# The last five steps of an image, issued in another order on every engine, in a fused attention-and-convolution kernel

## What is computed

```
xn = group_norm(x)                       # one group a channel
q, k, v = conv3(xn_windows, qw|kw|vw)    # 3x3, in windows of 16x16, then folded to 64 tokens of 128 features
q, k, v = layer_norm(q|k|v)
att = softmax(q k' + bias_table)         # 8 heads, 64 tokens
xr  = xn + unfold((att v) @ proj_w.T + proj_b)
y   = xr + conv3(gelu(conv3(xr, c1w, c1b)), c2w, c2b)      # 3x3 over the whole image
out = x + y
```

## Time and profile before

| | |
|---|---|
| time, median of 3 runs (lowest, highest) | 811.29 us (810.05, 811.31) |
| the profiled execution's own time | 810.2 us |
| its span in the trace | 808.4 us |
| mean granted TensorE clock | 0.993 |
| PE busy | 744.3 us, 92% |
| DVE busy | 657.2 us, 81% |
| ACT busy | 569.1 us, 70% |
| POOL busy | 491.9 us, 61% |

### The profile page before, as it was taken

One profiled execution on the slowest core, in us unless ns is written; L12 is line 12 of the kernel. 1 busy time (PEld: TensorE's weight loads), 2 busy tenths in 40 slices (PEclk: granted clock), 3 DMA queues, 4 the chain that ended last, 5 costly groups with the idle time before them and its releaser, 6 DMA issues.

```text
span 808.4 us, 18167 instructions
## 1 busy us (share of the span) xinstructions
PE 744.3 (92%) x5898; PEld 549.4 (68%) x5898; DVE 657.2 (81%) x2150; ACT 569.1 (70%) x1191; POOL 491.9 (61%) x1041
## 2 busy tenths in 40 slices
PE   0469999999899999999899999999999999999988
PEld 0247877777556778877555778777655688787753
DVE  6549889897859899897967989899775989887675
ACT  1399888767367988876547978876737788878630
POOL 6368778741457788763346777874244778886210
PEclk9999999999999999999999999999999999999999
DMA  7112331000013161000101332100101314000002
GB/s 266 59 30 60 96 144 60 2 1 23 38 65 97 33 239 44 18 1 1 59 33 54 110 125 116 60 1 2 56 5 66 98 32 135 2 2 2 2 1 104
DMA packets 17662, 47.32 MB, mean 59 GB/s; under 512 B 2080, under 2 KB 2720, under 8 KB 17568
## 3 DMA queue, kind: packets, MB, share of 16 engines
q1 hardware_dynamic: 17568, 46.15, 16.7%
HBM read 37.76 MB, written 8.39 MB: 57 GB/s over the span
## 4 chain that ended last, share of the span: by engine, by line
PE 67%; DVE 12%; ACT 9%; issue 5%; POOL 5%; DMA 0%; SPq 0%; POOLq 0%; ACTq 0%; DVEq 0%
PE y_ps L1015 18%; PE o_bank L1081 9%; PE s_ps L1056 8%; PE pt_ps L1069 7%; PE y_ps L982 4%; PE s_ps L1097 3%; PE t_ps L1040 3%; PE ox_ps L1138 3%; PE o_bank L1138 3%; PE pt_ps L1138 3%; PE s_ps L1138 3%; PE y_ps L1010 2%; DVE h_lo L505 2%; DVE h_hi L502 2%; ACT qk_n L855 1%
## 5 line engine op out<-in xcount | busy, mean ns | idle before, releaser
L743 POOL TENSOR_TENSOR sc<-sc,mx 128x512 f32<-128x512 f32 x128 | 133.7, 1044 | 59.9 <-DVE mx L568 59.9
L855 ACT ACTIVATE qk_n<-y_ps,ln_nr,ln_rs 128x128 f32<-128x128 f32 x256 | 104.4, 464 | 88.4 <-POOL ln_nr L733 88.2
L1015 PE MATMUL y_ps<-w_hi,x_hi 128*128 128x192 f16 (+1 forms) x512 | 147.2, 287 | 0.0
L1015 PE MATMUL y_ps<-w_hi,x_lo 128*128 128x192 f16 (+1 forms) x512 | 146.9, 287 | 0.0
L1015 PE MATMUL y_ps<-w_lo,x_hi 128*128 128x192 f16 (+1 forms) x512 | 146.7, 287 | 0.0
L541 DVE BATCH_NORM_STATS2 ln_st<-y_ps 128x6 f32<-128x128 f32 x384 | 88.8, 287 | 60.1 <-PE y_ps L1015 58.9
L1081 PE MATMUL o_bank<-v_bd,pt 128*128 128x66 f32 x1024 | 129.1, 269 | 3.9 <-DVE on L589 3.8
L1081 PEld LDWEIGHTS o_bank<-v_bd,pt 128*128 128x128 f32 x1024 | 124.4, 192 | 5.5 <-DVE pt L575 4.7
L730 POOL TENSOR_TENSOR ln_rs<-ln_ve,neg_half 128x3 f32<-128x3 f32 x128 | 113.4, 886 | 10.7
L870 ACT ACTIVATE sc<-sc 128x512 f32<-128x512 f32 x128 | 82.8, 647 | 39.3 <-POOL sc L743 39.3
L863 ACT ACTIVATE v_bd<-y_ps,ln_vs 128x128 f32<-128x128 f32 x256 | 105.2, 475 | 0.0
(11 more groups left out here) (190 smaller groups left out, 1607.7 us busy)
## 6 DMA issues: line engine op xcount, KB each, us to landing
xs<-in_x_sh_dram SPq DMA_DIRECT2D x32, 576.0 KB, 4.4
xst<-in_x_al_dram SPq DMA_DIRECT2D x16, 512.0 KB, 8.2
xf<-in_x_al_dram SPq DMA_DIRECT2D x32, 256.0 KB, 5.2
out_dram<-xf SPq DMA_DIRECT2D x32, 256.0 KB, 2.0
wst<-in_wqkv_dram SPq DMA_DIRECT2D x1, 768.0 KB, 4.2
w1s<-in_w_dram SPq DMA_DIRECT2D x1, 256.0 KB, 8.7
w2s<-in_w_dram SPq DMA_DIRECT2D x1, 256.0 KB, 8.7
biasS<-in_bias_t_dram SPq DMA_DIRECT2D x1, 256.0 KB, 9.6
```

The source lines that it names most:

```text
L743: pool.tensor_tensor(sc[i % 4][:, :, :, :], sc[i % 4][:, :, :, :], mx[i % 2][:, :, :].unsqueeze(2).to_broadcast([P, HP, TOK, 2]), ALU.subt ...
L855: ins = act.activation(qk_n[j][:, t, :].rearrange("p (h y x) -> p h y x", h=HEADS, y=2), by_head(y_ps[j][:, E * t:E * (t + 1)]), ACT.Identity,
L1015: ins = pe.matmul(y.rearrange("p (t e) -> p t e", t=3)[:, :, cols], xx[r % 2][:, s, a % 2, 2 * TS * (a // 2):2 * TS * (a // 2 + TS)], ww[: ...
```

## The change

Steps 32 to 36 are taken out of `steps` (which now ends at step 31), and each engine gets a function `tail` with the same work in another order. The bodies of the single jobs move into functions of their own and are otherwise as they were.

- PE: the transposes by key and outputs of the last pairs stand ahead of the tiles of the first convolution. Before, the order was c1(4), c1(5), by_key(30), outputs(29), project(6), c1(6), c1(7), by_key(31), outputs(30), by_feature(28), (29), c1(8), outputs(31), by_feature(30), c1(9), by_feature(31), project(7), c1(10), convolution of the next image's pair 0, c1(11), c1(12).
- The convolution of the next image's pair 0 stands ahead of c1(10) (`head` no longer issues it).
- The banks are dealt out anew: tiles 4 to 12 take `t_ps`, y0, y1, s0, s1, `t_ps`, s0, s1, `pt_ps`; project(6) takes the halves of `s_ps` like the projections before it, project(7) `ox_ps` and `o_bank`; c2(0) and c2(1) take s0 and s1. The waits follow.
- DVE: the copy, division and additions of the last pairs are spread between the `low` of the tiles: two `low` ahead of the last division, four between the next image's `row` and the last addition, four after it, then the border.
- ACT: the next image's `high` and the last `copy_ot` are interleaved with the read-outs of the tiles; `split(7)` stands ahead of the read-out of tile 9.
- POOL: `inverse` stands ahead of `split(5)`; the next image's four `low` stand between `split(6)` and `split(7)`, as before.

```diff
-            for i in range(HEAD.stop, PAIRS + 5):
+            for i in range(HEAD.stop, PAIRS):
...
-        c1_in = {28: (0,), 29: (1,), 30: (2,), 31: (3,), 32: (4, 5), 33: (6, 7), 34: (8,), 35: (9,), 36: (10,)}
+        c1_in = {28: (0,), 29: (1,), 30: (2,), 31: (3,)}
-        c1_bank = [t_bank if t == 10 else c_ps[t % 2 if t < 4 else (t + 2) % 4] for t in range(T1N)]
-        c2_bank = [c_ps[3], c_ps[2], pt_bank, o_bank[:, :], ox_ps[:, :], pt_bank, o_bank[:, :], ox_ps[:, :]]
-        proj_bank = [[s_ps[:, w, 256:512] for w in range(2)] for r in range(6)]
-        proj_bank += [[ox_ps[:, 0:256], t_bank[:, 0:256]], [ox_ps[:, 0:256], pt_bank[:, 0:256]]]
+        y0, y1, s0, s1 = c_ps
+        c1_bank = [y0, y1, y0, y1, t_bank, y0, y1, s0, s1, t_bank, s0, s1, pt_bank]
+        c2_bank = [s0, s1, pt_bank, o_bank[:, :], ox_ps[:, :], pt_bank, o_bank[:, :], ox_ps[:, :]]
+        proj_bank = [[s_ps[:, w, 256:512] for w in range(2)] for r in range(NROW - 1)]
+        proj_bank += [[ox_ps[:, 0:256], o_bank[:, 0:256]]]
...
-        low_in = {32: (0, 1, 2, 3), 33: (4, 5), 35: (6, 7, 8)}
...
+            def tail(b, p0, r0, followed):
+                copy_pt(30, p0)
+                normalise(29, p0)
+                if followed:
+                    row_scales(b + 1)
+                    start_scales(b + 1)
+                copy_pt(31, p0)
+                normalise(30, p0)
+                add_rows(6, b, r0)
+                low(b, 0)
+                low(b, 1)
+                normalise(31, p0)
+                if followed:
+                    for r in range(2):
+                        row(r, r0 + NROW)
+                for t in range(2, 6):
+                    low(b, t)
+                add_rows(7, b, r0)
+                for t in range(6, 10):
+                    low(b, t)
+                border(b, BORDER1, 1)
...
             def image(b, followed):
                 steps(pool, b, step, followed)
+                split(b, NROW - 2)
+                if followed:
+                    for r in range(2):
+                        for z in range(2):
+                            low(r, z, (b + 1) * PAIRS, (b + 1) * NROW)
                 split(b, NROW - 1)
...
+            def tail(b, p0, r0, followed):
+                copy_ot(6, p0, r0)
+                act.wait_ge(h_raw, b * RAW1 + RAW1)
+                for u in range(RAW1):
+                    gelu(b, u, hst[u][:, :, :])
+                c1_out(b, 4)
+                if followed:
+                    act.wait_ge(xn_scales, b + 2)
+                    for r in range(2):
+                        row(r, r0 + NROW, (b + 1) * (NROW // 2))
+                split(b, 6)
+                c1_out(b, 5)
+                c1_out(b, 6)
+                if followed:
+                    for z in range(2):
+                        high(0, z, p0 + PAIRS, r0 + NROW)
+                copy_ot(7, p0, r0)
+                c1_out(b, 7)
+                if followed:
+                    for z in range(2):
+                        high(1, z, p0 + PAIRS, r0 + NROW)
+                c1_out(b, 8)
+                split(b, 7)
+                for t in range(9, T1N):
+                    c1_out(b, t)
...
-                elif t < 6:
-                    pe.wait_ge(biased, b * PAIRS + PAIRS)
-                elif t < 8:
-                    pe.wait_ge(h_raw, b * RAW1 + (t - 3))
-                elif t == 10:
+                elif t == 4:
...
+                elif t < 7:
+                    pe.wait_ge(h_raw, b * RAW1 + (t - 2))
+                elif t < 9:
+                    pe.wait_ge(xr_added, b * NROW + NROW - 1 + ADD0)
+                elif t < 12:
+                    pe.wait_ge(gelu_done, b * T1N + {9: 5, 10: 8, 11: 9}[t])
                 else:
-                    pe.wait_ge(gelu_done, b * T1N + (t - 3))
+                    pe.wait_ge(pt_copied, b * PAIRS + PAIRS)
...
-                    pe.wait_ge(gelu_done, last * T1N + (7, 12)[m])
+                    pe.wait_ge(gelu_done, last * T1N + (6, 7)[m])
...
-                    pe.wait_ge(gelu_done, b * T1N + (10, 13)[t])
+                    pe.wait_ge(gelu_done, b * T1N + (11, 12)[t])
...
+            def tail(b, p0, r0, followed):
+                by_key(30, p0)
+                outputs(29, p0)
+                c1(b, 4)
+                by_key(31, p0)
+                outputs(30, p0)
+                project(6, p0, r0)
+                by_feature(28, p0, r0)
+                by_feature(29, p0, r0)
+                c1(b, 5)
+                outputs(31, p0)
+                c1(b, 6)
+                by_feature(30, p0, r0)
+                by_feature(31, p0, r0)
+                c1(b, 7)
+                project(7, p0, r0)
+                c1(b, 8)
+                c1(b, 9)
+                if followed:
+                    convolve(0, p0 + PAIRS, r0 + NROW, (b + 1) * (NROW // 2), b)
+                c1(b, 10)
```

More of the change, by code:

```diff
@@ L580, in step @@
                 if has(i - 3):
[L581 to L595, removed]
-                if i % 4 == 0 and i >= 8:
[L598 to L610, removed]
+                    normalise(i - 3, p0)
+                if i % 4 == 0 and i >= 8:
+                    add_rows((i - 8) // 4, b, r0)
                 if followed:
@@ new lines, in convolve @@
+            def convolve(m, p0, r0, rr0, last=None):
+                r, s = m // 4, m % 4
+                if s == 0:
+                    pe.wait_ge(xlo_done, (r0 + (r + 1)) * 2)
+                if m >= 2:
+                    pe.wait_ge(ln_v, p0 + (m - 1))
+                elif last is not None:
+                    pe.wait_ge(gelu_done, last * T1N + (6, 7)[m])
+                y = y_ps[m % 2][:, 0:QKV]
+                pe.matmul(y, ones_b[0:96, :], b_parts[0:96, :], start=True, stop=False)
+                for a in range(4):
+                    cols = {0: slice(0, E // 2), 3: slice(E // 2, E)}.get(a, slice(0, E))
+                    for xx, ww in ((x_hi, w_hi), (x_hi, w_lo), (x_lo, w_hi)):
+                        ins = pe.matmul(y.rearrange("p (t e) -> p t e", t=3)[:, :, cols],
+                                        xx[r % 2][:, s, a % 2, 2 * TS * (a // 2):2 * TS * (a // 2 + TS)],
+                                        ww[:, a, :].rearrange("p (t e) -> p t e", t=3)[:, :, cols],
+                                        start=False, stop=(a == 3 and xx is x_lo))
+                ins.then_inc(conv_done, 1)
@@ new lines, in by_key @@
+            def by_key(m, p0, last=None):
+                pe.wait_ge(exped, p0 + (m + 1))
+                if m == 0 and last is not None:
+                    pe.wait_ge(y_ready, last * T2N + 6 + 1)
+                if m >= 1:
+                    pe.wait_ge(pt_copied, p0 + m)
+                for g in range(HP):
+                    ins = pe.transpose(pt_ps[:, g, :], sc[m % 4][:, g, :, :].rearrange("p k w -> p (k w)"),
+                                       idf[:, :])
+                ins.then_inc(ptr_done, 1)
@@ new lines, in outputs @@
+            def outputs(m, p0, last=None):
+                pe.wait_ge(pt_copied, p0 + (m + 1))
+                if m == 0 and last is not None:
+                    pe.wait_ge(y_ready, last * T2N + 7 + 1)
+                if m >= 1:
+                    pe.wait_ge(normed, p0 + m)
+                for g in range(HP):
+                    ins = pe.matmul(o_ps[:, g, :, :].rearrange("p w d -> p (w d)"), pt[m % 2][:, g, :],
+                                    v_bd[m % 8][:, g, :, :].rearrange("p w d -> p (w d)"),
+                                    start=True, stop=True)
+                ins.then_inc(pv_done, 1)
@@ new lines, in project @@
+            def project(r, p0, r0):
+                pe.wait_ge(ot_copied, r0 + (r + 1))
+                if r < NROW - 1:
+                    pe.wait_ge(biased, p0 + min(4 * r + 9, PAIRS))
+                else:
+                    pe.wait_ge(normed, p0 + PAIRS)
+                for par in range(2):
+                    for w in range(2):
+                        half = slice(64 * w, 64 * w + 64)
+                        ins = pe.matmul(proj_bank[r][w].rearrange("p (i m j) -> p i m j", i=TS, m=NPAIR),
+                                        projg[half, par, :],
+                                        ot[r % 2][half, :].rearrange("p (m a i j) -> p a i m j", m=NPAIR, a=2, i=TS)[
+                                            :, par, :, :, :], start=par == 0, stop=par == 1)
+                ins.then_inc(proj_done, 1)
@@ L1021, in step @@
+            def step(i, p0, h0, r0, rr0, row0, b=None, followed=False, last=None):
+                if has(i + 5) and not (i == HEAD.start and last is not None):
+                    convolve(i + 5, p0, r0, rr0, last)
                 if last is not None:
@@ L1102, in step @@
-                if i == PAIRS + 4:
-                    for t in c1_in[i]:
-                        c1(b, t)
+                    by_key(i - 2, p0, last)
+                if has(i - 3):
+                    outputs(i - 3, p0, last)
```

(2 more changed lines are left out.)

170 lines of the change are left out of this document (55 added, 115 removed).

## The result

| | before | changed |
|---|---|---|
| median | 811.3 us (810.05 to 812.55, 4 runs) | 803.38 us (802.73 to 804.8, 4 runs) |
| ratio, 95% interval | | 0.9905 (0.9883 to 0.9926) |
| profiled execution | 810.2 us | 804.8 us |
| its span | 808.4 us | 803.0 us |

The account below looks back on a forecast made before the run. PE, busy 92% of the span, loses time before c2(0), whose start DVE's list would set after the change. Three images at 2.2 us plus 0.9 make 7.5 us: 810.2 - 7.5 = 802.7 us, range 798 to 807.5 us.

Parts of the forecast that it names:

- The mark: Start of c2(0), with PE full for 38 us behind it: 214.1 against 216.27 us, a gain of 2.2 us.
- DVE's list: DVE's work up to the border's end: 214.68 - 3.2 + 1.9 + 0.7 = 214.1 us, setting c2(0).
- the row chain: Last addition to xr, then ACT's and POOL's split, for c1(11): ready at 208.6 us, no longer holding PE.
- PE's list: PE's work from 187.64 us to c2(0): 23.7 plus waits 0.9 and 0.5, ending 212.7; rival that it sets c2(0): 798.5 us, 12%.
- The blocks by POOL: DVE's `low` held up under POOL's x_lo and split(7): 4.1 us against 3.4 before, +0.7 us.
- at nothing: POOL's inverse moved ahead of split(5), charged nothing, since no tile before c1(5) needs that row late.
- freak delays: Case that DVE's long instructions aren't POOL's blocks: border would end near 210 us and PE's 212.7 would hold.
- the early start: DVE's list begins with copy(30) at 189.1 us, not at 192.28: -3.2 us.
- The head: Behind c2(0): pair 3's convolution keeps at least 0.6 of 2.2 us slack, nothing charged; late-DVE rival includes slack used up, 15%.
- The clock: Rival: granted clock falls behind c2(0)'s new wait, 1.6 us an image, 807.5 us, 13%; three low stretches, 817.1 us, 5%.
- Image 3: Last image, without inverse, scales or x_lo: gain 0.6 to 1.1, say 0.9 us.
- DVE's 3.2 us of idleness: DVE idles 3.23 us until POOL's `inverse` at 192.28, then works 22.4 us in a row; this idleness is cut.

Follow-up runs that it names:

- without columns: Changed kernel with six of the eight column memsets of the first border left out: 798.67 us, ratio 0.9845.
- small x_lo: Changed kernel with POOL's four x_lo instructions between images cut to 2 of 128 columns: 798.12 us, ratio 0.9839.
- border 8: Changed kernel, first border after 8 tiles, low(8), low(9) behind next head's pair 0 statistics, low(10) to low(12) and second border behind pair 1's: 800.22 us.
- the run with fillers: Kernel before with eight matmuls that nobody reads behind c1(8) in images 0 to 2: 811.27 us, ratio 0.9995.
- The early inverse by itself: Kernel before with only POOL's inverse moved ahead of split(5): 808.22 us, ratio 0.9958.
- the fastest variant: The even border kernel with c1(4) again ahead of by_key(30): 796.14 us, ratio 0.9816.
- the even border: Changed kernel, first border after 8 tiles, low(8) to low(11) behind next head's pair 0 statistics, low(12) and second border behind pair 1's: 798.59 us.
- The late inverse: Changed kernel with POOL's inverse back behind split(5): 804.77 us, ratio 0.9927.

## Why the prediction was right, step by step

- **The mark.** c2(0) at 215.92 - 1.68 = 214.2 us where 214.1 was forecast. That DVE's list and no longer the row chain sets it, with PE waiting 1.4 to 1.9 us, came as forecast (1.82): the mechanism was right, not only the number; the runs without columns and with small x_lo show it by taking DVE's load away.
- **PE's list.** Waits at the start of 0.7 us and 0.1, the latter ahead of outputs(29), against 0.9; at project(7) 0.33 against 0.5; project(7) at 201.1 (without the shift) against 201.0; the list's end at 214.1 - 1.7 = 212.4 against 212.7.
- **DVE's list.** Copy(30) at 190.81 - 1.68 = 189.1, as forecast. Waits 0.5, 0.3, 0.2 and 0.4 = 1.4 us against 1.9 (the forecast's own five terms make 1.8). The last addition at 206.2 against 205.9, where the forecast's terms, 198.9 + 3.6 + 3.1, make 205.6.
- **The blocks by POOL.** The five long instructions (1.33 twice, 1.29, 1.28, 1.25) are 0.8 to 0.9 us each above their normal lengths (0.56 for h_lo, 0.39 for h_hi), 4.2 us against 4.1. The four of the kernel before, booked at 3.4, make 3.3 by the same count, so the new order costs 0.9 us there, not 0.7. A sixth block was not forecast: POOL's inverse ahead of split(5), moved "at nothing", put split(5) beside DVE's scales, 0.2 us. That the blocks are POOL's doing, and no freak delays, the run with small x_lo shows: the block goes with the POOL instruction and stays with the split that was left. The forecast weighed this as the port lock of the Trainium skill, SBUF — State Buffer, section "SBUF: two separate sides". The trace agrees with a full block (0.56 us becomes 1.33); the port itself no run here shows.
- **Luck in the sum.** The waits were booked 0.5 us too high. The blocks were booked 0.4 us too low, and 0.1 us of small gaps was not booked. These errors cancel: of the 3.2 us that the early start brings, 1.9 + 0.7 = 2.6 us were forecast to be lost again, and 2.65 were. The hit to 0.1 us is owed to that.
- **The head** kept its slack: 38.38 us busy of 38.40. The run with border 8 shows how near the edge was.
- **The clock** stayed at 1.0 in the last steps and behind them, in all images: the single waits of 1.8 us did not bring it down. The forecast counted the 1.6 us of low clock as gone from PE's list, but let DVE's list set the time. That it was no gain of its own is shown by the run with fillers.
- **Image 3** gained 1.0 us against 0.9. PE's waits there, 1.1 and 0.9 us before, became 0.7 and 0.1.
- **What was mis-sized.** The gain of 2.2 us an image; it is 2.0. And DVE's 3.2 us of idleness, which the forecast took for the source of the gain, do not hang on `inverse` alone. The early inverse by itself brings 1.0 us; with the rest of the new order, it can be undone at no cost. Copy(30) no longer stands behind the scales in the new order, and the waits for PE behind it absorb a late inverse.

## What to carry to other kernels

Write down each engine's list between two marks and ask which list ends last after the change, not which wait disappears: here PE's list ended 3.9 us earlier (216.3 to 212.4) and the gain was 2.0, because DVE's list ended 1.8 us behind it. The list that ends last can be shortened by moving work past the mark into slots where that engine idles. Moved in too large a block, it gave back 0.8 of 2.0 us here; spread over the idle slots, nothing. A low clock on an engine that waits afterwards anyway cost nothing here.

## What the runs showed that was not expected

- A low clock in the first 65 us comes and goes between executions. The profiled executions of the kernel before, of the one with fillers and of the fastest variant have 1.00 between 30 and 60 us, that of the changed kernel 0.88, the others 0.91 to 0.94. From the start of DVE's first `bn_stats` to image 0's copy of pair 29 it is 171.0 us in those three and 172.0 to 173.1 us in the others, the changed kernel's being the longest. That first `bn_stats` itself starts between 16.2 and 17.4 us. Together this shifts image 0's last steps by up to 2.5 us. So single executions are not comparable below 2 us; distances from image to image are, to 0.1 us (189.20 and 189.21 us in two executions of the changed kernel). In the profiled execution of the even border the clock also stood at 0.95 from 45 to 212 us, so its distances are taken behind that. First `bn_stats`, before and changed:

```profile
16.64 4.83 DVE L450 BATCH_NORM_STATS2 gst<-xst 128x6 f32<-128x512 f32 x8
```

```profile
16.24 4.83 DVE L450 BATCH_NORM_STATS2 gst<-xst 128x6 f32<-128x512 f32 x8
```

- A wait need not cost what it lasts. The late inverse held DVE for 1.13 us and cost less than 0.1 us from image to image, because four later waits of DVE gave way to it and one block by POOL fell away.
- Not every DVE instruction is held up by POOL. In the kernel before, the last division, which reads a PSUM bank, kept its length (0.59 us) beside POOL's x_lo of 203.24 to 208.50 us. By which rule some are spared, no run here tells.

```profile
205.10 0.59 DVE L589 TENSOR_TENSOR on<-o_bank,rs 64x128 f32<-64x128 f32 x2
```

- The cost of a border memset goes with its rows: those of 32 partitions by 50 rows come every 0.32 us with 0.10 us recorded, those by 40 rows every 0.27 us with 0.09 recorded. Most of it is listed as "issue", in front of the next instruction.
